# Last cross attention: a mask bias over 32 rows per group, and four heads exponentiated by ScalarE straight from the scores

## The chip, the cores and the metric

The kernel runs on one core of a Trainium2 chip. The metric is the device time of the whole program in microseconds (us); the kernel before has a median of 1068.53 us over 3 runs (1067.91 to 1072.55). Five engines work side by side, each in its own program order: TensorE (PE, matmuls and transposes; PEld is its weight load), VectorE (DVE), ScalarE (ACT), GpSimd (POOL) and SyncE (SP, which issues transfers). They meet in semaphores.

## The reference

A decoder of four layers, each a gated cross attention on 77 context tokens followed by a gated feed-forward part. The input x is 4 batches of 512 tokens of width 128; every cross attention has 16 heads. The change touches the cross attention of layer 3:

```python
qh = _rope((q @ w_q + b_q) split into 16 heads of 8)
kh = _rope((k @ w_k + b_k) split into 16 heads of 8)
vh = (v @ w_v + b_v) split into 16 heads of 8
scores = jnp.einsum('bhqd,bhkd->bhqk', qh, kh) / math.sqrt(dk)
scores = jnp.where(mask, scores, jnp.finfo(scores.dtype).min)   # mask: (4, 1, 1, 77)
attn = jax.nn.softmax(scores, axis=-1)
out = jnp.einsum('bhqk,bhkd->bhqd', attn, vh)
x = x + jnp.tanh(g_xattn[3]) * (out merged @ w_o + b_o)
```

## The kernel before

The 2048 tokens are 16 tiles of 128 (NT = 16, four tiles TB of each batch). For a tile of the last cross attention (called X3 in the code) the scores of all heads are 128 x 1232 (16 heads of 77 keys). They stand in four PSUM banks, four heads (GK = 308 columns) each: RG = 4 groups, and group g uses rows 32g to 32g+31 of the queries and of a block-diagonal key matrix, so a score matmul has 32 rows.

Each engine runs a loop over the tiles with an order written out by hand: `skewed_loop(engine, steps, ...)` runs the steps once for each k, a step with lag j being about tile k - j. For X3, in this order:

- PE: `score(k)`, `late_fold(k)` (for the first tiles only), `product(k-3)`, `turn_probs(k-2)`.
- ACT: `stage(k+1)` (copies the tile's queries to `qs`), `evacuate(k-3)` (four copies of the transposed probabilities from PSUM to `PT`), `exponent(k-1)`. As `exponent` is one tile ahead of PE's turning and `evacuate` is written before it, the exponentials of tile t stand behind the copies of tile t-2.
- DVE: `largest(k)` (maximum of each head, read from the scores), `shift(k)` (scores less the maximum, to `att`), `total(k-1)` (sum of each head), `invert(k-1)`, `update(k-3)` (adds the result to x).
- POOL: `normalize(k)` (probabilities times the reciprocal of the sum), which PE turns in `turn_probs`.

`score(k)` writes the scores in the same four banks for every tile. It waits for `staged` (ACT has copied the queries) and for `shifted` (DVE has read the scores of tile k-1 for the last time). In X3 four more matmuls add the mask's bias `nb3` to the scores: each multiplies the 128 x 128 identity `identb` with the group's 308 columns. The four tiles of a batch share the bias, and all 128 rows of it are alike. The exponential applies the scale 1/sqrt(8).

The second cross attention (X1) already has a split: there ACT takes six heads one by one (line 1349, input from SBUF, with the maximum as bias and the sum as accumulated output) and ten heads in one instruction (line 1352).

Of the kernel before, what the change touches and what calls it, by code (L numbers as in the profile page):

```python
# [6 lines left out]
BF16 = mybir.dt.bfloat16  # L7
# [3 lines left out]
ALU = mybir.AluOpType  # L11
# [5 lines left out]
KEYS = 77  # L17
H, HD = 16, 8
HD2 = 64
P = 128  # L20
# [185 lines left out]
def build(nc, x_in, packed, w_ffn1, w_moe, w_mla, split2, w_ffn3, rope, mask1, mask3, normed1, sums1, out):  # L206
    ctx = ExitStack()
    with ctx:
# [28 lines left out]
        mask3_u8 = sb("mask3_u8", [P, CK], U8)  # L237
        identb = sb("identb", [P, P], BF16)
        cmaskb = sb("cmaskb", [P, HK], BF16)
        tg = sb("tg", [P, 8])  # L240
        stats = sb("stats", [P, NT, 6])
        mv = sb("mv", [P, NT, 2])
# [212 lines left out]
        def over_group_keys(a):  # L455
            return a.rearrange("p (g h) -> p g h", g=RG).unsqueeze(3).to_broadcast([P, RG, H // RG, KEYS])

        SPLIT = H - 6

        def over_keys(a):  # L460

            return a.unsqueeze(2).to_broadcast([P, H, KEYS])

        def over_part(a):
            return a.unsqueeze(2).to_broadcast([P, SPLIT, KEYS])

        def fold_of(u):

# [128 lines left out]
        def _(pe):  # L597
# [124 lines left out]
            def cross(s):  # L722


                n0 = tiles_before(s)

                def score(t):
                    pe.wait_ge(staged, t.n + n0 + 1)

                    if s in (X1, X2):  # L730
                        pe.wait_ge(scores_read, t.n + (LAYER[s] - 1) * NT + 1)
                    else:
                        pe.wait_ge(shifted, t.n + n0 + 1)
                    causal = s == X2 and t.k % TB == 0
                    if s == X2:
                        for c in range(3):
                            a, z = c * BANK, min((c + 1) * BANK, HK)
                            m = mm(flat[:, a:z], qs[:, t.slot(2), :], batch(KBD, t.group)[:, a:z],
                                   start=True, stop=not causal)
                            if causal:  # L740
                                m = mm(flat[:, a:z], identb[:, :], cmaskb[:, a:z], start=False, stop=True)
                    else:
                        for g in range(RG):
                            rows = slice(32 * g, 32 * g + 32)
                            m = mm(ps[:, g, 0:GK], qs[rows, t.slot(2), :], batch(KBG, t.group)[rows, :],
                                   start=True, stop=s != X3)
                        if s == X3:
                            for g in range(RG):
                                m = mm(ps[:, g, 0:GK], identb[:, :], batch(nb3, t.group)[:, g * GK:(g + 1) * GK],
                                       start=False, stop=True)  # L750
                    m.then_inc(scores, 1)

                def turn_probs(t):
                    pe.wait_ge(probs, t.n + n0 + 3)
                    if isinstance(t.n, int) and t.n == 0 and s in FOLD:
                        pe.wait_ge(vw_sb, (FOLD[s] + 1) * B + 1)
                    if s == X1 and t.n == 0:
                        pe.wait_ge(turned_sb, TURN0[X1] + 2 * B + 1)
                    for k in range(3):

                        pe.wait_ge(probsT, t.n * 3 + 3 * n0 + k + 1)
                        if s == X0 and k == 1 and 1 <= t.n <= 2 * PARTS:
                            pe.wait_ge(side_sb, side_piece(t.n - 1) + 1)
                        for c in range(4 * k, min(4 * k + 4, NC)):
                            m = P if c < NC - 1 else LAST
                            q = pe.transpose(ps[0:m, (3 if s == X2 else 4) + k, (c % 4) * P:(c % 4 + 1) * P],  # L766
                                             att[:, 2 + t.slot(2), c * P:c * P + m], ident)
                        q.then_inc(probsT_ps, 1)

                def late_fold(t):  # L770
                    if s == X1 and t.n + 2 < B:
                        turn_q1(t.n + 2)
                    if s == X3 and t.n == 0:
                        rotate(B - 1)
                        pe.wait_ge(roped, B - 1)
                        pe.wait_ge(q_sb, 2 * B)
                    if s == X3 and t.n + 2 < B:
                        fold_values(s, w(f"{LAYER[s]}wo"), t.n + 2)

                def product(t):  # L780

                    if s == X0 and t.n in (0, 2 * TB, 3 * TB):
                        pe.wait_ge(side_sb, side_piece(PARTS * (t.n // TB - 1) - 1) + 1 if t.n else side_query(3) + 1)
                    if s == X1 and t.n == 0:
                        pe.wait_ge(values_in, 16 * len(SHARES))
                    if s == X3 and t.n == 0:
                        pe.wait_ge(roped, B)
                    pe.wait_ge(x_new, t.n + XNEW0[s] - (1 if s == X2 else 0))
                    for k in range(3):
                        pe.wait_ge(probsT, t.n * 3 + 3 * n0 + k + 4)  # L790
                        for c in range(4 * k, min(4 * k + 4, NC)):
                            m = P if c < NC - 1 else LAST
                            q = mm(attended(s, t), PT[0:m, t.slot(2), c, :],  # L793
                                   batch(VW, t.group)[0:m, c * D:(c + 1) * D], start=(c == 0), stop=(c == NC - 1))
                    q.then_inc(attn_out, 1)

                if s != X2:
                    pe.wait_ge(kbd, KEYED[s] + 1)
                if s == X2:
                    pe.wait_ge(vw_bo, 1)  # L800
                elif s == X3:
                    pe.wait_ge(vw_sb, FOLD[s] * B + 3)
                if s == X2:
                    pe.wait_ge(bf_done, 2)
                if s == X3:
                    pe.wait_ge(tables_set, 4)
                if s == X0:
                    return score, product, turn_probs
                skewed_loop(pe, [(score, 0), (late_fold, 0), (product, 3), (turn_probs, 2)], NT, TB if s == X2 else NT)
# [459 lines left out]
        def _(act):  # L1269
# [58 lines left out]
            def cross(s, scale):  # L1328
# [4 lines left out]
                def stage(t):  # L1333

                    act.wait_ge(scores, t.n + n0 + 1)
                    q = FT[:, bass.ds(t.n * P, P)]
                    if s == X1:
                        go(qs[:, t.slot(2), :], q, ACT.Copy, scale=HD ** -0.5).then_inc(staged, 1)
                    else:
                        go(qs[:, t.slot(2), :], q, ACT.Copy).then_inc(staged, 1)  # L1340

                def exponent(t):
                    if s == X1:
                        act.wait_ge(rowmax, t.n + n0 + 1)
                        act.wait_ge(probsT_ps, t.n * 3 + 3 * n0 + 3)
                        wait(act, recip, t.n + n0 - 1)
                        for h in range(SPLIT, H):
                            keys = slice(h * KEYS, (h + 1) * KEYS)
                            go(att[:, 2 + t.slot(2), keys], att[:, t.slot(2), keys], ACT.Exp,
                               bias=mx[:, t.slot(2), h:h + 1], accum_out=rs[:, t.slot(2), h:h + 1])  # L1350
                        act.wait_ge(shifted, t.n + n0 + 2)
                        go(att[:, 2 + t.slot(2), 0:SPLIT * KEYS], att[:, t.slot(2), 0:SPLIT * KEYS], ACT.Exp)\  # L1352
                            .then_inc(expd, 1)
                        return
                    act.wait_ge(shifted, t.n + n0 + 2)

                    act.wait_ge(probsT_ps, t.n * 3 + 3 * n0 + 3)
                    go(att[:, 2 + t.slot(2), :], att[:, t.slot(2), :], ACT.Exp, scale=scale).then_inc(expd, 1)  # L1358
# [389 lines left out]
        def _(pool):  # L1748
# [218 lines left out]
            for b in range(B):  # L1967
                tt(heads(VBD3_at[b]), v3_s[:, b * KEYS:(b + 1) * KEYS].unsqueeze(1).to_broadcast([P, H, KEYS]),
                   over_keys(w("hm")), ALU.mult).then_inc(vbd, 1)
            pool.wait_ge(ld["e"], 32)  # L1970
            for b in range(B):
                t = pool.tensor_scalar(heads(nb3[:, b, :]),
                                       mask3_u8[:, b * KEYS:(b + 1) * KEYS].unsqueeze(1).to_broadcast([P, H, KEYS]),
# [14 lines left out]
        def _(dve):  # L1988
# [88 lines left out]
            def cross(s):  # L2077
# [14 lines left out]
                def largest(t):  # L2092
# [7 lines left out]
                    top = mx[:, t.slot(2), :]  # L2100
                    if s not in (X1, X2):
                        top = top.rearrange("p (g h) -> p g h", g=RG)
                    v.tensor_reduce(top, src, AX.X, ALU.max, negate=s == X1).then_inc(rowmax, 1)

                def shift(t):

                    a = heads(att[:, t.slot(2), :])
                    dve.wait_ge(rowmax, t.n + n0 + 1)
                    if s == X1:
                        tt(a[:, 0:SPLIT, :], a[:, 0:SPLIT, :], over_part(mx[:, t.slot(2), 0:SPLIT]), ALU.add).then_inc(shifted, 1)  # L2110
                    elif s == X2:
                        tt(a, a, over_keys(mx[:, t.slot(2), :]), ALU.subtract).then_inc(shifted, 1)  # L2112
                    else:
# [2 lines left out]

                def total(t):
                    dve.wait_ge(expd, t.n + n0 + 3)
                    n = SPLIT if s == X1 else H
                    v.tensor_reduce(rs[:, t.slot(2), 0:n], heads(att[:, 2 + t.slot(2), :])[:, 0:n, :], AX.X, ALU.add)\  # L2120
                        .then_inc(rowsum, 1)

# [710 lines left out]
```

## Time and profile before

| | before |
|---|---|
| median of 3 runs | 1068.53 us |
| profiled execution, its own time | 1071.78 us |
| its span, first to last instruction | 1069.7 us |
| PE busy over the span | 927.7 us (87%) |
| DVE busy over the span | 785.9 us (73%) |
| ACT busy over the span | 556.0 us (52%) |
| POOL busy over the span | 489.7 us (46%) |
| first score matmul of X3 | at 932.84 us |
| last update of x in X3 | at 1024.86 us |

The tile loop of X3 thus takes some 92 us of the 1069.7. Times within the program are us from the start of the span. A number in brackets at the end of a timeline row is the time in which the engine sat idle before the row, with what released it.

### The profile page before, as it was taken

How to read it: one execution, taken by the hardware profiler on the slowest of the kernel's cores; microseconds unless marked ns; L12 is line 12 of the kernel's file. 1: busy time of each engine (PE TensorE's matmuls, PEld its weight loads, DVE VectorE, ACT ScalarE, POOL GpSimd, SP SyncE). 2: the span in 40 equal slices, each digit the busy share in tenths (PEclk: the TensorE clock that was granted, in tenths of full speed). 3: DMA queues.
4: the chain of work that ended last, by engine and by line, in shares of the span. 5: the costliest groups of instructions: out<-in, count | busy, mean ns of one | idle time of the engine just before them, and what ended most of it. 6: DMA issues, size and time to landing. Idle time of an engine off the chain costs nothing.

```text
span 1069.7 us, 19683 instructions
## 1 busy us (share of the span) xinstructions
PE 927.7 (87%) x6397; PEld 663.6 (62%) x6401; DVE 785.9 (73%) x2080; ACT 556.0 (52%) x1493; POOL 489.7 (46%) x451
## 2 busy tenths in 40 slices
PE   6998985988778999859997598988989999989987
PEld 4787633767577989737775243434447677667773
DVE  5889999999756777769996476776834644589962
ACT  3675456886434445724443166666764333455523
POOL 6444553555066565625566766574530600034420
PEclk9999896999889999979999568999999999999989
DMA  9300000000211111410000322122002000000001
GB/s 326 141 1 1 2 6 1 1 1 1 41 38 41 33 44 34 119 54 1 0 1 15 98 71 84 50 83 57 23 12 88 1 1 2 1 1 1 1 1 39
DMA packets 29828, 40.55 MB, mean 38 GB/s; under 512 B 11468, under 2 KB 25036, under 8 KB 29228
## 3 DMA queue, kind: packets, MB, share of 16 engines
q1 hardware_dynamic: 27244, 34.28, 10.3%
q0 software_dynamic: 2496, 5.16, 1.9%
q8 instruction: 48, 0.79, 0.3%
q14 instruction: 40, 0.33, 0.1%
HBM read 31.44 MB, written 7.82 MB: 37 GB/s over the span
## 4 chain that ended last, share of the span: by engine, by line
PE 26%; issue 14%; POOL 7%; DVE 5%; ACT 3%; SPq 1%; DMA 0%; POOLq 0%; DVEq 0%; ACTq 0%
POOL att L1783 5%; PE ps L829 4%; PE ps L1163 4%; PE ps L819 4%; PE ps L1135 3%; PE ps L1147 3%; PE ps L793 1%; SPq L570 1%; PE ps L1249 1%; PE ps L1256 1%; DVE rs L2120 1%; PE ps L1101 0%; DVE stats L1997 0%; PE ps L607 0%; PE ps L1263 0%
## 5 line engine op out<-in xcount | busy, mean ns | idle before, releaser
L1783 POOL TENSOR_TENSOR att<-att,ri 128x1232 f32<-128x1232 f32 x64 | 169.3, 2645 | 192.4 <-DVE ri L2126 192.4
L793 PE MATMUL ps<-VW,PT 128*128 128x128 f32 (+3 forms) x1280 | 159.1, 280 | 16.6 <-DVE x L2141 15.1
L793 PEld LDWEIGHTS ps<-VW,PT 128*128 128x128 f32 (+1 forms) x1280 | 149.9, 193 | 34.7 <-DVE x L2141 27.0
L1366 ACT ACTIVATE PT<-ps 128x512 f32<-128x512 f32 x128 | 70.5, 594 | 90.0 <-PE ps L766 89.2
L766 PE MATMUL ps<-W,att 128*128 128x128 f32 (+1 forms) x640 | 87.2, 283 | 16.8 <-POOL att L1783 15.3
L1757 POOL TENSOR_TENSOR rstd<-ve,minus_half 128x4 f32<-128x4 f32 x38 | 38.9, 1040 | 114.1 <-DVE ve L2012 97.5
L900 PE MATMUL ps<-PT,att 128*128 128x128 f32 x624 | 79.9, 283 | 9.9 <-issue 9.0
L766 PEld LDWEIGHTS ps<-W,att 128*128 128x128 f32 (+1 forms) x640 | 73.0, 143 | 22.9 <-POOL att L1783 16.1
L829 PEld LDWEIGHTS ps<-U,att 128*128 128x128 f32 x512 | 66.3, 191 | 33.1 <-issue 29.1
L2577 DVE CUSTOM_DVE_ANT_0 C<-ps,cmaskb 128x512 bf16<-128x512 f32 (+1 forms) x128 | 71.1, 555 | 20.2 <-PE ps L1135 17.4
L2577 DVE CUSTOM_DVE_ANT_0 U<-ps,cmaskb 128x384 bf16<-128x384 f32 (+1 forms) x128 | 54.0, 422 | 43.1 <-PE ps L1135 42.9
L2120 DVE TENSOR_REDUCE rs<-att 128x16 f32<-128x1232 f32 (+1 forms) x64 | 83.6, 1306 | 1.2 <-ACT att L1352 0.8
L900 PEld LDWEIGHTS ps<-PT,att 128*128 128x128 f32 x624 | 75.0, 197 | 14.0 <-issue 12.8
L1135 PE MATMUL ps<-W,U 72*128 72x512 bf16 (+3 forms) x256 | 68.7, 344 | 16.4 <-DMA W<-split 9.5
L2273 DVE SCALAR_TENSOR_TENSOR U<-ps,w_all,U 128x128 f32<-128x128 f32 x128 | 36.0, 344 | 57.1 <-PE ps L829 57.0
L1414 ACT ACTIVATE att<-ps 128x512 f32<-128x512 f32 x64 | 38.1, 597 | 74.9 <-PE ps L819 74.9
L1147 PE MATMUL ps<-U,W 108*128 108x512 bf16 (+3 forms) x256 | 72.3, 323 | 5.4 <-ACT VW L1672 2.1
L1358 ACT ACTIVATE att<-att 128x1232 f32<-128x1232 f32 x48 | 59.2, 1234 | 33.5 <-DVE att L2112 33.5
L829 PE MATMUL ps<-U,att 128*128 128x128 f32 x512 | 67.6, 276 | 3.1 <-DVE U L2273 2.4
L819 PE MATMUL ps<-FT,U 128*128 128x512 f32 x128 | 65.0, 595 | 0.0
L1440 ACT ACTIVATE FT<-ps,att 128x128 f32<-128x128 f32 x156 | 44.7, 375 | 35.2 <-PE ps L900 29.1
L1840 POOL DMA_INDIRECT PT<-normed,VBD x39 | 42.0, 1078 | 40.0 <-DVE VBD L2376 28.5
(430 smaller groups left out, 2120.6 us busy)
## 6 DMA issues: line engine op xcount, KB each, us to landing
U<-in_ffn SPq DMA_DIRECT2D x1, 6176.0 KB, 23.4
U<-split SPq DMA_DIRECT2D x144, 32.0 KB
W<-split SPq DMA_DIRECT2D x144, 32.0 KB
W<-in_packed SPq DMA_DIRECT2D x1, 2162.5 KB, 23.9
U<-in_ffn SPq DMA_DIRECT2D x1, 2060.0 KB, 9.5
U<-in_moe SPq DMA_DIRECT2D x1, 2048.0 KB, 7.4
split<-VBD SPq DMA_DIRECT2D x4, 384.0 KB, 2.9
split<-W SPq DMA_DIRECT2D x4, 384.0 KB, 2.8
```

What stands on the lines that cost most here:

```text
L766: q = pe.transpose(ps[0:m, (3 if s == X2 else 4) + k, (c % 4) * P:(c % 4 + 1) * P], att[:, 2 + t.slot(2), c * P:c * P + m], ident)
L793: q = mm(attended(s, t), PT[0:m, t.slot(2), c, :], batch(VW, t.group)[0:m, c * D:(c + 1) * D], start=(c == 0), stop=(c == NC - 1))
L819: mm(ps[:, u % 2, :], W1M[:, e, j * P:(j + 1) * P], FT[:, cols(c)], start=True, stop=True)\
L829: t = mm(ps[:, 4 + e % 2, i * D:(i + 1) * D], hh[:, u % 2, i * P:(i + 1) * P], W2M[:, e, j, :], start=(j == 0 and i == 0), stop=(j == J2 - ...
L900: t = mm(ps[:, 2 + 2 * k + a, c * P:(c + 1) * P], chosen1[:, k, at:at + P], pickedT[:, k, :], start=True, stop=True)
L1135: mm(ps[:, 2 * (t % RINGS), 0:(i + 1) * P], queries[0:STACK, n % HOLD, g, i * P:(i + 1) * P], keys[0:STACK, n % HOLD, g, 0:(i + 1) * P], s ...
L1147: mm(ps[:, 2 * (t % RINGS) + 1, 0:S - j * P], keys[0:rows, n % HOLD, g, j * P:(j + 1) * P], queries[0:rows, n % HOLD, g, j * P:S], start=T ...
L1358: go(att[:, 2 + t.slot(2), :], att[:, t.slot(2), :], ACT.Exp, scale=scale).then_inc(expd, 1)
L1366: go(PT[:, t.slot(2), 4 * k:4 * k + 4, :].rearrange("p c n -> p (c n)"), ps[:, k0 + k, :], ACT.Copy).then_inc(probsT, 1)
L1783: tt(p, p, over_keys(ri[:, t.slot(2), :]), ALU.mult).then_inc(probs, 1)
L2120: v.tensor_reduce(rs[:, t.slot(2), 0:n], heads(att[:, 2 + t.slot(2), :])[:, 0:n, :], AX.X, ALU.add)\
L2577: v.tensor_tensor_reduce(unused[t % 2][:, 0:z], ps[:, 2 * (t % RINGS), 0:z], visible[:, S - z:S], -1.0, -NEG, ALU.add, ALU.min, nm[:, n % ...
```

## The change

There are two parts. First, the mask's bias: the stationary operand is no longer the identity but 32 rows of a constant `part_ones` (all elements 1/32), against the same 32 rows of the bias; the sum of 32 equal rows over 32 is the bias. POOL sets the constant once, before the loop.

Second, the exponentials: ACT scales the queries when it stages them and no longer in the exponential. DVE takes the maximum negated, as in X1, and shifts three groups (12 heads, 924 columns). The last four heads, which are the whole of bank 3, are exponentiated by ACT one by one from PSUM, with the maximum as bias and the sum accumulated; DVE sums only 12 heads. As ACT now reads scores, the next tile's `score` waits for it as well (`scores_read`).

```diff
-        SPLIT = H - 6
+        SPLIT = {X1: H - 6, X3: H - H // RG}
...
                     else:
                         pe.wait_ge(shifted, t.n + n0 + 1)
+                        if s == X3:
+                            pe.wait_ge(scores_read, t.n + (LAYER[s] - 1) * NT + 1)
...
                             for g in range(RG):
-                                m = mm(ps[:, g, 0:GK], identb[:, :], batch(nb3, t.group)[:, g * GK:(g + 1) * GK],
-                                       start=False, stop=True)
+                                rows = slice(32 * g, 32 * g + 32)
+                                m = mm(ps[:, g, 0:GK], part_ones[rows, :],
+                                       batch(nb3, t.group)[rows, g * GK:(g + 1) * GK], start=False, stop=True)
...
-                    if s == X1:
+                    if s in (X1, X3):
                         go(qs[:, t.slot(2), :], q, ACT.Copy, scale=HD ** -0.5).then_inc(staged, 1)
...
                 def exponent(t):
-                    if s == X1:
+                    if s in SPLIT:
                         act.wait_ge(rowmax, t.n + n0 + 1)
                         act.wait_ge(probsT_ps, t.n * 3 + 3 * n0 + 3)
                         wait(act, recip, t.n + n0 - 1)
-                        for h in range(SPLIT, H):
+                        n = SPLIT[s]
+                        for h in range(n, H):
                             keys = slice(h * KEYS, (h + 1) * KEYS)
-                            go(att[:, 2 + t.slot(2), keys], att[:, t.slot(2), keys], ACT.Exp,
-                               bias=mx[:, t.slot(2), h:h + 1], accum_out=rs[:, t.slot(2), h:h + 1])
+                            own = slice((h - n) * KEYS, (h - n + 1) * KEYS)
+                            e = go(att[:, 2 + t.slot(2), keys], att[:, t.slot(2), keys] if s == X1 else ps[:, RG - 1, own],
+                                   ACT.Exp, bias=mx[:, t.slot(2), h:h + 1], accum_out=rs[:, t.slot(2), h:h + 1])
+                        if s == X3:
+                            e.then_inc(scores_read, 1)
                         act.wait_ge(shifted, t.n + n0 + 2)
-                        go(att[:, 2 + t.slot(2), 0:SPLIT * KEYS], att[:, t.slot(2), 0:SPLIT * KEYS], ACT.Exp)\
-                            .then_inc(expd, 1)
+                        go(att[:, 2 + t.slot(2), 0:n * KEYS], att[:, t.slot(2), 0:n * KEYS], ACT.Exp).then_inc(expd, 1)
                         return
...
             pool.wait_ge(ld["e"], 32)
+            pool.memset(part_ones[:, :], 1.0 / 32).then_inc(zeros_set, 1)
+            pool.wait_ge(zeros_set, B + 4)
...
-                    v.tensor_reduce(top, src, AX.X, ALU.max, negate=s == X1).then_inc(rowmax, 1)
+                    v.tensor_reduce(top, src, AX.X, ALU.max, negate=s in SPLIT).then_inc(rowmax, 1)
...
+                    elif s == X3:
+                        g = RG - 1
+                        m = mx[:, t.slot(2), 0:SPLIT[s]].rearrange("p (g h) -> p g h", g=g).unsqueeze(3)
+                        tt(by_group(att[:, t.slot(2), :])[:, 0:g], group_scores(s)[:, 0:g],
+                           m.to_broadcast([P, g, H // RG, KEYS]), ALU.add).then_inc(shifted, 1)
...
-                    n = SPLIT if s == X1 else H
+                    n = SPLIT.get(s, H)
```

ACT's queue in the X3 loop, one turn before (`PT` are the copies of `evacuate`, `att` the exponential, lines 1369 and 1370 its last two copies; the bracket names the semaphores that a row waits for):

```order
L1364 REGISTER_ALU [waits attn_out]
L1366 ACTIVATE PT<-ps 128x512 [waits probsT_ps]
L1364 REGISTER_ALU
L1366 ACTIVATE PT<-ps 128x512 [waits probsT_ps]
L1364 REGISTER_ALU
L1369 ACTIVATE PT<-ps 128x128 [waits probsT_ps]
L1370 ACTIVATE PT<-ps 80x128
L1357 ISA [waits shifted]
L1358 ACTIVATE att<-att 128x1232 [waits probsT_ps]
```

The same turn now:

```order
L1371 REGISTER_ALU [waits attn_out]
L1373 ACTIVATE PT<-ps 128x512 [waits probsT_ps]
L1371 REGISTER_ALU
L1373 ACTIVATE PT<-ps 128x512 [waits probsT_ps]
L1371 REGISTER_ALU
L1376 ACTIVATE PT<-ps 128x128 [waits probsT_ps]
L1377 ACTIVATE PT<-ps 80x128
L1349 ISA [waits rowmax]
L1355 ACTIVATE att,rs<-ps,mx 128x77 [waits recip,probsT_ps]
L1355 ACTIVATE att,rs<-ps,mx 128x77 x3
L1360 ACTIVATE att<-att 128x924 [waits shifted]
```

The four copies stay ahead; between them and the large exponential stand four exponentials that read the scores from PSUM.

PE's queue at the end of the turning and the start of the next tile's scores, before (`KBD,qs` are the score matmuls, `C,identb` the mask's, `VW,PT` the product):

```order
L766 MATMUL ps<-W,att 128x128 [waits probsT]
L766 MATMUL ps<-W,att 80x128
L745 MATMUL ps<-KBD,qs 128x308 [waits shifted,q_staged]
L745 MATMUL ps<-KBD,qs 128x308 x3
L749 MATMUL ps<-C,identb 128x308 x4
L793 MATMUL ps<-VW,PT 128x128 [waits probsT,x_new]
```

And now:

```order
L770 MATMUL ps<-W,att 128x128 [waits probsT]
L770 MATMUL ps<-W,att 80x128
L748 MATMUL ps<-KBD,qs 128x308 [waits scores_read,shifted,q_staged]
L748 MATMUL ps<-KBD,qs 128x308 x3
L753 MATMUL ps<-C,part_ones 128x308 x4
L797 MATMUL ps<-VW,PT 128x128 [waits probsT,x_new]
```

Nothing changes place on PE; the first score matmul has one more semaphore to wait for, and the mask's matmuls another stationary operand.

## Rows read from the trace of the kernel before

**Rows 1.** Window: length; busy (x count) of PE, PEld, DVE, ACT, POOL; PE clock.
```profile
951.00:1012.00 61.00, 59.68 (x523) 49.28 (x522) 57.78 (x62) 32.30 (x71) 27.01 (x12) 1.00 0.01 2
```
**Rows 2.** Timeline of X3's loop, two tiles: start us, duration us, engine, line, what.
```profile
974.74 0.25 DVE L2126 RECIPROCAL ri<-rs 128x16 f32<-128x16 f32 x1
975.07 2.25 POOL L1783 TENSOR_TENSOR att<-att,ri 128x1232 f32<-128x1232 f32 x1 [2.98 <-DVE ri L2126]
...
978.79 0.80 PE L745 MATMUL ps<-KBD,qs 32*128 32x308 f32 x8
...
979.52 0.70 PE L749 MATMUL ps<-C,identb 128*128 128x308 bf16 x4
979.53 1.24 ACT L1358 ACTIVATE att<-att 128x1232 f32<-128x1232 f32 x1
...
980.06 2.39 PE L793 MATMUL ps<-VW,PT 128*128 128x128 f32 x20
980.26 1.44 DVE L2103 TENSOR_REDUCE mx<-ps 128x16 f32<-128x1232 f32 x1 [0.37 <-PE ps L749]
...
981.74 1.44 DVE L2114 TENSOR_TENSOR att<-ps,mx 128x1232 f32<-128x1232 f32 x1
...
982.29 1.26 PE L766 MATMUL ps<-W,att 128*128 128x128 f32 x10
...
983.10 1.43 DVE L2120 TENSOR_REDUCE rs<-att 128x16 f32<-128x1232 f32 x1
...
983.48 0.80 PE L745 MATMUL ps<-KBD,qs 32*128 32x308 f32 x8
...
984.56 0.25 DVE L2126 RECIPROCAL ri<-rs 128x16 f32<-128x16 f32 x1
```
**Rows 3.** Groups by line and form, DVE of X3, ACT of X1.
```profile
L2114 DVE TENSOR_TENSOR att<-ps,mx 128x1232 f32<-128x1232 f32 x16 | 23.1, 1441 | 0.5
...
L2120 DVE TENSOR_REDUCE rs<-att 128x16 f32<-128x1232 f32 x16 | 22.8, 1426 | 0.0
...
L1349 ACT ACTIVATE att<-att,mx 128x77 f32<-128x77 f32 x96 | 33.1, 358 | 0.0
L1349 ACT ACTIVATION_READ_ACCUMULATOR att<-att,mx 128x1 f32 x96 | 19.2, 200 | 0.0
```
**Rows 4.** Timeline of ACT in X1: first of six heads, and what follows the sixth.
```profile
194.83 0.36 ACT L1349 ACTIVATE att<-att,mx 128x77 f32<-128x77 f32 x1
...
196.89 0.84 ACT L1352 ACTIVATE att<-att 128x770 f32<-128x770 f32 x1
```
**Rows 5.** Timeline of PE in the third cross attention: scores over 128 rows.
```profile
493.22 2.23 PE L738 MATMUL ps<-KBD,qs 128*128 x6
495.29 0.94 PE L793 MATMUL ps<-VW,PT 128*128 x7
```
**Rows 6.** Timeline of X3: score of tiles 1, 3 and 15, first exponential, last update.
```profile
937.52 0.80 PE L745 MATMUL ps<-KBD,qs 32*128 32x308 f32 x8
...
939.11 1.24 ACT L1358 ACTIVATE att<-att 128x1232 f32<-128x1232 f32 x1
...
948.63 1.32 PE L745 MATMUL ps<-KBD,qs 32*128 32x308 f32 x8
...
1008.35 0.80 PE L745 MATMUL ps<-KBD,qs 32*128 32x308 f32 x8
...
1024.86 0.35 DVE L2141 SCALAR_TENSOR_TENSOR x<-ps,tg,x 128x128 f32<-128x128 f32 x1 [2.00 <-PE ps L793]
```
**Rows 7.** Timeline of PE after two idle stretches of over 2 us.
```profile
472.99 2.34 PE L738 MATMUL ps<-KBD,qs 128*128 128x512 f32 x6 [2.59 <-ACT qs L1340]
...
946.30 2.40 PE L766 MATMUL ps<-W,att 128*128 128x128 f32 x10 [2.43 <-POOL att L1783]
```
**Rows 8.** Windows of PE: us, busy (x count), granted clock, DMA.
```profile
946.00:950.00 4.00, 3.70 (x19) 0.57 0.00 0
...
474.00:478.00 4.00, 1.33 (x5) 1.00 0.00 0
```

More of the change, by code:

```diff
@@ L239, in build @@
         cmaskb = sb("cmaskb", [P, HK], BF16)
+        part_ones = sb("part_ones", [P, P], BF16)
         tg = sb("tg", [P, 8])
@@ L464, in over_part @@
         def over_part(a):
-            return a.unsqueeze(2).to_broadcast([P, SPLIT, KEYS])
+            return a.unsqueeze(2).to_broadcast([P, SPLIT[X1], KEYS])
         def fold_of(u):
@@ L2109, in shift @@
                     if s == X1:
-                        tt(a[:, 0:SPLIT, :], a[:, 0:SPLIT, :], over_part(mx[:, t.slot(2), 0:SPLIT]), ALU.add).then_inc(shifted, 1)
+                        n = SPLIT[s]
+                        tt(a[:, 0:n, :], a[:, 0:n, :], over_part(mx[:, t.slot(2), 0:n]), ALU.add).then_inc(shifted, 1)
+                    elif s == X3:
[3 more added lines that the diff above has]
+                           m.to_broadcast([P, g, H // RG, KEYS]), ALU.add).then_inc(shifted, 1)
                     elif s == X2:
```

## Prediction

> **What bounds the kernel now.** I first read the windows over X3's tile loop. The reader is to see there that two engines are nearly full: in 61 us PE is busy 59.68 and DVE 57.78, while ACT has 32.30 and POOL 27.01, and PE's clock is 1.00, the 2.4 GHz level [rows 1]. So DVE time taken away gives something only if PE can go faster too, and an idle stretch put into PE's queue costs nearly its full length.
>
> The second view is the timeline of the loop [rows 2]. PE's turn (scores, mask, product of tile k-3, turning of tile k-2) has no wait between 978.79 and 983.48: 4.69 us, PE's floor. DVE's strand takes two tiles: invert at 974.74, POOL's normalize at 975.07, the turning, scores at 978.79, mask at 979.52, maximum at 980.26, shift at 981.74, sum at 983.10, invert again at 984.56. That is 9.82 us for two tiles, 4.91 each. From the score of tile 3 at 948.63 to that of tile 15 at 1008.35 there are 12 turns in 59.72 us, 4.98 each [rows 6]: now PE is the last, now the strand.
>
> The third thing is ACT's place. When the next score starts at 978.79, the turning is over; ACT finishes its four copies of the turned tile and starts its exponential only at 979.53, 0.74 us later [rows 2]. Before, no score waited for that: `score` waited for DVE's shift, done long before.
>
> **The change part by part.**
>
> *The four heads' exponentials and the new wait.* In X1 six such exponentials take from 194.83 to 196.89, 0.343 us each from start to start, with the reading of the accumulator inside [rows 4]. Four of them: three steps of 0.343 and the last one's own 0.358 [rows 3], 1.39 us. They stand behind the copies, and `score` of the next tile waits for the last of them. A turn of PE thus gets a tail that nothing hides, since PE is in order and the product and the turning stand behind the waiting score: 0.74 for the copies, 1.39 for the heads, and a handover. For that the rows show 0.08 from the reciprocal's end (974.99) to POOL's start (975.07) and 0.04 from the mask's end to the maximum; I take 0.1. The tail is 2.23 us.
> These exponentials read PSUM, which no row of before shows with an accumulator. Bounds: from below the element rate of the whole exponential, 1.24 us for 1232 columns [rows 2], 0.31 for 308; from above four times exponential and accumulator one after the other, 4 x (0.358 + 0.200) = 2.23 [rows 3]. I take 1.39, as it is the same instruction with another source.
> The Trainium skill, "ScalarE: Activation LUTs", section "Rules for kernel authors", budgets about 0.3 us per ACTIVATE and 0.83 ns per element: an estimate from that page is 0.364 us for a head and 1.46 for four; the X1 rows say 0.343 and 1.37. By the page the end would be 0.07 x 13, about 1 us later.
>
> *The mask over 32 rows per group.* The mask's phase is 979.52 to 980.06, 0.54 us [rows 2]. What four row groups side by side are worth, scores show: the third cross attention streams 2 x 1232 columns through all rows in 2.07 us (493.22 to 495.29) [rows 5], X3 the same 2 x 1232 columns over 32 rows per group in 0.73 (978.79 to 979.52) [rows 2], a factor of 2.8. So the mask goes to 0.19, a gain of 0.35. Bounds: no gain at all, and 0.54 / 4 = 0.135, a gain of 0.41.
>
> *DVE's work.* Shift and sum have 924 instead of 1232 columns: 1441 and 1426 ns [rows 3] become about 1080 and 1070 in proportion, gains of 0.36 each per tile. Bounds: nothing, and all of it on the path, 0.72 x 16 = 11.5 us. In the loop I cost them at nothing, as DVE then waits for PE.
>
> *The rest.* The scale in ACT's staging and the negated maximum are in instructions that run anyway. The constant is one memset of 128 columns on POOL ahead of the loop; POOL is half idle there. Nothing, at most 1 us.
>
> **The new turn.** PE's work is 4.69 - 0.35 = 4.34, and the tail 2.23: 6.57 us. The tail closes a ring: score(k), product, turning of k-2, copies of k-2, heads of k, score(k+1). No buffer opens it, for the scores of all tiles share four banks. The other ring, DVE's strand, becomes 9.82 + 2.23 - 0.35 - 0.72 = 11.0 for two tiles, 5.5 each, and is hidden.
>
> **The sum.**
> - Beginning: the score of tile 1 started at 937.52. Now it waits for the heads of tile 0, which start where the exponential started, 939.11 [rows 6]: 939.11 + 1.39 + 0.10 = 940.60, +3.1. From there to the score of tile 3 the way leads over the maximum, shift, sum, normalize and turning of tile 0, and then the tail: + 2.23 - 0.35 - 0.72, and - 1.14 because I book the slow clock below (2.40 for ten transposes at 946.30 [rows 7] against 1.26 at 982.29 [rows 2]). That is 0. Together +3.1.
> - Tiles 3 to 15: 12 x 6.57 = 78.8 instead of 59.7: +19.1.
> - End: from 1008.35 to 1024.86 [rows 6] DVE's strand ends it. It gets shorter by 0.35 (mask), 0.36 (shift) and two sums (0.72), and I give 0.2 back for the last tile's exponentials, which now come after the heads: -1.2.
> - Sum at the fast clock: +21.0.
> - Clock: PE now has some 14 idle stretches of about 2.2 us. The rows show both outcomes for such a stretch: after 2.43 us at 946.30 the clock was at 0.57 over the next 4 us, and after 2.59 us at 472.99 it stayed at 1.00 [rows 7, 8]. At 0.57, 3.4 of the 4 us are at 1.2 GHz, half of which is lost: 1.7 us for a fall. I take one stretch in four: 3.5 x 1.7 = +6.
>
> That is +27. The profiled execution had 1071.78 us (span 1069.7 and 2.1 around it); it becomes 1099. It stood 3.25 above the median of the runs, so I forecast 1096 us.
>
> **The rivals.**
> - *B: the clock falls in most turns.* Mechanism: a turn idles a third of the time, so PE slips to 1.2 GHz after nearly every tail. For it: the fall at 946.30 [rows 7]. Against it: the 472.99 row. If each of 14 falls costs 1.7, the sum is 21 + 24 = 45, 1114 us; if they last longer than one piece of work, 1125 and more. The Trainium skill, "TensorE: Matmul & The Clock Gate", section "A second HAM failure mode: psum-queue depth-cycling", describes a kernel in which small idle times between bursts make the clock go up and down all the time; by that rule B is the case, and the traces so far show falls here and there only.
> - *C: the tail is shorter.* If the four exponentials from PSUM run near the element rate (0.31 us instead of 1.39), the turn is 5.5 us, where DVE's ring stands as well: 12 x 0.5 at the tiles, 2 at the beginning, -1 at the end, and few falls: +7 to +12, 1076 to 1081 us. Against it: 0.343 in every X1 tile.
> - *D: faster.* The ring would not close if the heads ended no later than the turning: then their start would have to be 1.5 us before the next score and not 0.74 behind it. From that point on the gains decide: PE's floor 4.34, DVE's strand 9.82 - 0.35 - 0.72 = 8.75 for two, 4.4 a turn; 12 x (4.98 - 4.4) = 7, and 1 at the end: 1060.5. For it is that DVE is 95% busy. Against it: the copies stand in front of the heads in ACT's queue, and they need the turning.
> - *E: the mask alone misses.* With no gain from it, A has 0.35 x 13 = 4.6 more: 1101. It is inside A's range.
>
> **How the numbers follow.** A, the tail with some falls: 0.66, its own range 1087 to 1104 (no fall 1089.5; mask and heads as bounded nearby). B 0.17, C 0.11, D 0.04, and 0.02 for an end within 0.5% of before (5.3 us, what a measurement of this kernel can hardly tell from no change), which needs C and a tail that mostly hides. The range of 1080 to 1117 holds A, the better end of B and the worse end of C. Faster 0.04, same 0.02, slower 0.94.
>
> **What would show it.** In the trace of the changed kernel: PE's score rows of X3 released by ACT (the exponential of one head from PSUM), with some 2.2 us idle before most of them; 6.6 us from score to score; the heads 0.34 apart, and the first 0.74 behind the turning's end; mask phase 0.2; shift near 1.08, sum near 1.07, and a DVE that now waits over 2 us a tile for the mask; the clock at half in a few stretches. The forecast is wrong if scores start right behind the turning (D), if the heads' rows are closer than 0.3 apart (C), or if the transposes of most tiles take 2.4 instead of 1.26 us (B). X1, X2 and all stages ahead of X3 should be as before; a difference there would be another cause.

## The result, and the profile after

The changed kernel takes 1101.25 us in the median of 5 runs (1100.50 to 1102.83), beside 1068.87 us for the kernel before (5 runs). The ratio is 1.0298, with a 95% interval of 1.0275 to 1.0320: about 3% slower, 32.4 us in the medians. The profiled execution took 1100.5 us with a span of 1098.5, 28.8 more than the span before; the execution profiled before had been 2.9 us above its median, which is most of the difference between 28.8 and 32.4.

The page's first part is of little help: PE has 930.1 us (85%) busy now, DVE 775.2 (71%), ACT 572.5 (52%). Work hardly changed. The tile loop of X3 shows what did. First the window that answers to [rows 1] (the same columns), here over the loop and over its undisturbed middle:

```profile
951.00:1038.00 87.00, 59.17 (x514) 50.35 (x512) 51.66 (x64) 47.98 (x180) 28.70 (x13) 0.94 0.00 1
975.00:1012.00 37.00, 24.30 (x232) 20.74 (x233) 21.29 (x26) 21.94 (x83) 13.09 (x6) 1.00 0.00 1
```

PE was busy 98% of the loop and DVE 95%; now each is below 70% of it (24.30 and 21.29 of 37 us in the middle). A loop in which no engine is full must be held by waits, and the waits view (waiting engine and line, releaser: total us, times, longest) names them:

```profile
DVE mx L2112 <- PE ps L753: 38.1, 13, 5.4
ACT PT L1373 <- PE ps L770: 34.2, 14, 4.1
...
PE ps L748 <- ACT att L1355: 27.8, 13, 2.2
```

PE's scores wait for ACT's last head in every turn, ACT for PE's turning, DVE for the scores. The timeline of one turn, which answers to [rows 2] (start, duration, engine, line; in brackets the idle time and its releaser), shows the order of the joints:

```profile
996.78 0.80 PE L748 MATMUL ps<-KBD,qs 32*128 32x308 f32 x8 [2.14 <-ACT att L1355]
...
997.37 0.34 PE L753 MATMUL ps<-C,part_ones 32*128 32x308 bf16 x4
...
997.64 2.50 PE L797 MATMUL ps<-VW,PT 128*128 128x128 f32 x20
997.75 1.44 DVE L2112 TENSOR_REDUCE mx<-ps 128x16 f32<-128x1232 f32 x1 [2.46 <-PE ps L753]
...
999.23 1.12 DVE L2124 TENSOR_TENSOR att<-ps,mx 128x924 f32<-128x924 f32 x1
...
999.98 1.26 PE L770 MATMUL ps<-W,att 128*128 128x128 f32 x10
...
1000.61 1.08 ACT L1373 ACTIVATE PT<-ps 128x512 f32<-128x512 f32 x2 [2.45 <-PE ps L770]
...
1001.74 0.28 ACT L1377 ACTIVATE PT<-ps 80x128 f32<-80x128 f32 x1
1001.90 0.33 ACT L1355 ACTIVATE att<-ps,mx 128x77 f32<-128x77 f32 x1
...
1002.80 0.34 ACT L1355 ACTIVATE att<-ps,mx 128x77 f32<-128x77 f32 x1
1003.00 0.22 ACT L1355 ACTIVATION_READ_ACCUMULATOR att<-ps,mx 128x1 f32 x1
1003.10 0.99 ACT L1360 ACTIVATE att<-att 128x924 f32<-128x924 f32 x1
...
1003.37 0.80 PE L748 MATMUL ps<-KBD,qs 32*128 32x308 f32 x8 [2.14 <-ACT att L1355]
```

From score to score it is 6.59 us. The last copy of the turned tile (1001.74), the first head (1001.90), the fourth (1002.80) and the next score (1003.37) stand one after the other. DVE finished with these scores at 1000.35, the end of its shift, 3 us before the next score began. The granted clock answers to [rows 8] (windows of PE, same columns):

```profile
930.00:948.00 18.00, 12.23 (x74) 0.81 0.00 1
948.00:975.00 27.00, 20.27 (x148) 0.81 0.00 1
975.00:1012.00 37.00, 24.30 (x232) 1.00 0.00 1
1012.00:1022.00 10.00, 7.86 (x61) 0.83 0.01 2
1022.00:1038.00 16.00, 9.52 (x94) 1.00 0.00 0
```

A mean of 0.81 is a clock at its lower level, 1.2 GHz, for 38% of the stretch. In all it stood there for some 20 us of X3, against some 3.4 us before [rows 8]. Single turns show it: the six turns from 977.00 to 1016.56 take 6.59 to 6.60 us each, but three turns of the loop take 8.2, 8.1 and 8.2 us, such as this one, whose scores begin at the lower clock (1.41 instead of 0.80 us):

```profile
1016.56 1.41 PE L748 MATMUL ps<-KBD,qs 32*128 32x308 f32 x8 [2.14 <-ACT att L1355]
1017.72 0.51 PE L753 MATMUL ps<-C,part_ones 32*128 32x308 bf16 x4
1018.15 3.32 PE L797 MATMUL ps<-VW,PT 128*128 128x128 f32 x20
1021.31 1.26 PE L770 MATMUL ps<-W,att 128*128 128x128 f32 x10
1024.71 0.80 PE L748 MATMUL ps<-KBD,qs 32*128 32x308 f32 x8 [2.14 <-ACT att L1355]
```

The groups that answer to [rows 3], with busy us, mean ns and idle us before them:

```profile
L2124 DVE TENSOR_TENSOR att<-ps,mx 128x924 f32<-128x924 f32 x16 | 17.9, 1120 | 0.5
L2135 DVE TENSOR_REDUCE rs<-att 128x12 f32<-128x924 f32 x16 | 17.7, 1106 | 0.2 <-ACT att L1360 0.2
...
L1355 ACT ACTIVATE att<-ps,mx 128x77 f32<-128x77 f32 x64 | 19.8, 336 | 0.0
L1355 ACT ACTIVATION_READ_ACCUMULATOR att<-ps,mx 128x1 f32 x64 | 14.0, 219 | 0.0
```

DVE did get its relief (1441 and 1426 ns before). Between tile 3 and tile 15 PE never waits for DVE any more, so there the relief is worth nothing; only the end of X3, where DVE's work is the path, gets it.

Cut along X3, in us, from the two traces:

| stretch | before | after | difference |
|---|---|---|---|
| start to the score of tile 0 | 932.85 | 931.40 | -1.5 |
| score of tile 0 to that of tile 3 | 15.78 | 22.70 | +6.9 |
| tile 3 to tile 15 (12 turns) | 59.72 | 83.86 | +24.1 |
| tile 15 to the last update of x | 16.51 | 15.32 | -1.2 |
| from there to the end | 44.84 | 45.22 | +0.4 |
| span | 1069.7 | 1098.5 | +28.8 |

The first row is no effect that can be told from the spread: in the two later traces of the changed kernel the score of tile 0 starts at 937.12 and 930.70, so the part ahead of X3 differs by 6 us between executions of the same kernel.

### The profile page after: what moved, and what is told of

Read it like the earlier page. It is cut to its first block, busy times and chain, and to the rows that moved or that the text cites. A ratio compares the mean times of both kernels' runs of the same rounds, so it can differ in the third digit from the quotient of the medians.

```text
span 1098.5 us, 19828 instructions
## 1 busy us (share of the span) xinstructions
PE 930.1 (85%) x6401; PEld 667.0 (61%) x6401; DVE 775.2 (71%) x2080; ACT 572.5 (52%) x1621; POOL 488.7 (44%) x452
## 4 chain that ended last, share of the span: by engine, by line
PE 35%; issue 8%; POOL 6%; ACT 6%; DVE 3%; SPq 1%; DMA 0%; ACTq 0%; POOLq 0%; DVEq 0%
PE ps L833 5%; PE ps L823 5%; PE ps L1167 4%; PE ps L797 4%; POOL att L1790 4%; PE ps L1139 4%; PE ps L1151 3%; ACT att L1355 2%; PE ps L748 1%; PE ps L673 1%; PE ps L770 1%; PE ps L1260 1%; PE ps L1253 1%; ACT PT L1373 1%; PE ps L608 0%
## 5 line engine op out<-in xcount | busy, mean ns | idle before, releaser
L797 PE MATMUL ps<-VW,PT 128*128 128x128 f32 (+3 forms) x1280 | 162.7, 284 | 14.7 <-DVE x L2156 12.6
L797 PEld LDWEIGHTS ps<-VW,PT 128*128 128x128 f32 (+1 forms) x1280 | 152.8, 196 | 35.9 <-DVE x L2156 23.3
L770 PEld LDWEIGHTS ps<-W,att 128*128 128x128 f32 (+1 forms) x640 | 72.4, 142 | 20.9 <-POOL att L1790 13.3
L2112 DVE TENSOR_REDUCE mx<-ps 128x16 f32<-128x1232 f32 x32 | 46.1, 1441 | 55.1 <-PE ps L753 43.7
L2135 DVE TENSOR_REDUCE rs<-att 128x16 f32<-128x1232 f32 (+2 forms) x64 | 78.5, 1226 | 1.4 <-ACT att L1360 1.0
L1421 ACT ACTIVATE att<-ps 128x512 f32<-128x512 f32 x64 | 38.1, 597 | 76.6 <-PE ps L823 76.6
L748 PE MATMUL ps<-KBD,qs 32*128 32x308 f32 x384 | 43.9, 530 | 35.1 <-ACT att L1355 33.8
```

Source lines behind the costliest of these rows:

```text
L797: q = mm(attended(s, t), PT[0:m, t.slot(2), c, :], batch(VW, t.group)[0:m, c * D:(c + 1) * D], start=(c == 0), stop=(c == NC - 1))
```

## The experiments

My theory had three parts: the loss is the wait of `score` for ACT's heads, which puts copies, heads and PE's turn in series; the rest of it is the clock, which PE's idle stretches pull down; and the mask part is a gain. The rivals: ACT's longer queue or reading PSUM costs the time wherever it stands; the clock's falls are hidden by the ring; the mask's form costs something or is hidden.

The kernel before has another median in each group of runs measured together (1059.91, 1069.70 and 1073.50 us), so whole times are compared as ratios to the runs of before beside them. The finer measures, both from each trace, are the mean turn of tiles 3 to 15 and the stretch from the first score of X3 to the last update of x.

| kernel | ratio to before, 95% interval | mean turn | X3, first score to last update |
|---|---|---|---|
| before | 1 | 4.98 | 92.0 |
| the changed kernel | 1.0298 (1.0275 to 1.0320) | 6.99 | 121.9 |
| mask alone | 0.9973 (0.9954 to 0.9993) | 4.82 | 89.6 |
| heads before the copies | 1.0179 (1.0141 to 1.0217) | 6.16 | 113.1 |
| PE filled | 1.0221 (1.0182 to 1.0259) | 6.51 | 112.9 |
| heads from SBUF, mask | 0.9937 (0.9911 to 0.9963) | 4.62 | 85.6 |
| the changed kernel, second time | 1.0294 (1.0252 to 1.0337) | 6.99 | 122.0 |
| heads from PSUM alone | 1.0294 (1.0250 to 1.0339) | 7.30 | 128.4 |
| heads from SBUF, old mask | 0.9959 (0.9942 to 0.9977) | 4.83 | 89.2 |
| six heads from SBUF, mask | 0.9931 (0.9906 to 0.9956) | 4.51 | 84.3 |
| the changed kernel, third time | 1.0265 (1.0234 to 1.0296) | 6.99 | 122.0 |
| heads from PSUM alone, again | 1.0293 (1.0252 to 1.0334) | 7.04 | 119.4 |

**The mask alone** (e1): the kernel before with

```diff
-                                m = mm(ps[:, g, 0:GK], identb[:, :], batch(nb3, t.group)[:, g * GK:(g + 1) * GK],
+                                rows = slice(32 * g, 32 * g + 32)
+                                m = mm(ps[:, g, 0:GK], part_ones[rows, :],
+                                       batch(nb3, t.group)[rows, g * GK:(g + 1) * GK], start=False, stop=True)
```

Expected: 

> The kernel before with the mask's bias over 32 rows per group alone; the exponentials stay as before. In the trace after, score and mask phases together take 0.86 us instead of 1.27. My theory (the loss comes wholly from the wait for ACT's heads; the mask part is a gain) expects DVE's two-tile strand to shrink by about 0.4, a turn of 4.7 to 4.8 us instead of 4.98, and 3 us less than before: 1065 to 1067 us. The rival that the mask's new form costs something (a slower or later matmul over 32 rows) expects 1070 us or more.

Measured: 1056.28 us against 1059.91, 2.9 us less by the ratio, with an interval that excludes 1. A turn took 4.82 us. The mask part is a gain, as the prediction had it, and the rival that it costs something is out.

**The heads before the copies** (e3): in ACT's list of steps

```diff
-                    steps = [(stage_last, -1), (evacuate, 3), (exponent, 1), (late_fold, 0)]
+                    steps = [(stage_last, -1), (last_heads, 1), (evacuate, 3), (exponent, 1), (late_fold, 0)]
```

`last_heads` being the four exponentials taken out of `exponent`.

Expected: 

> The changed kernel with ACT's four exponentials of heads from PSUM put ahead of the four copies of evacuate (they still wait for the turning of tile t-2, whose buffer they write). My theory (a ring PE - copies - heads - next score, each link in series) expects the tail of 2.2 us to lose the copies' 0.6 to 0.7 us, a turn of about 5.9 instead of 6.6 us, and 8 to 10 us less than the changed kernel: 1091 to 1093 us. The rival that the price lies in the exponentials' own length or in reading PSUM beside DVE expects no change: 1101 us.

Measured: the ratio is 1.0179. Against the changed kernel's three ratios (1.0265 to 1.0298) that is 9 to 13 us less; the changed kernel ran in other groups, so X3 is the closer measure, and it is 8.8 us shorter. PE's idle time before a score, from the timeline:

```profile
980.94 0.33 ACT L1354 ACTIVATE att<-ps,mx 128x77 f32<-128x77 f32 x1 [2.30 <-PE ps L770]
...
981.85 0.33 ACT L1354 ACTIVATE att<-ps,mx 128x77 f32<-128x77 f32 x1
...
982.15 1.09 ACT L1390 ACTIVATE PT<-ps 128x512 f32<-128x512 f32 x2
...
982.42 0.80 PE L748 MATMUL ps<-KBD,qs 32*128 32x308 f32 x8 [1.52 <-ACT att L1354]
```

It is 1.52 instead of 2.14 us: the copies' share is gone from the tail. The turns are 5.96 to 6.14 us after the first, 6.02 in the mean, 0.58 less than the undisturbed 6.60 and near the expected 5.9. Over 12 turns that is 7.0 us; another 3.0 us of the loop are clock, as only one turn was long and not three; and the end became 1.2 us longer. The same exponentials, with the same source and the same number, cost less when they stand elsewhere. So it is the place in the queue that counts; the rival (no change) falls.

**PE filled** (e4): between the two waits of `score` in X3

```diff
                         pe.wait_ge(shifted, t.n + n0 + 1)
                         if s == X3:
+                            for _ in range(32):
+                                mm(ps[:, 0, 0:P], identb[:, :], identb[:, :], start=True, stop=True)
                             pe.wait_ge(scores_read, t.n + (LAYER[s] - 1) * NT + 1)
```

Expected: 

> The changed kernel with 32 idle matmuls of 128 columns (into bank 0, whose scores DVE has read, before the wait for ACT; they add nothing to the result) in each turn of PE in X3, some 1.8 us of the 2.14 us in which PE idles. My theory says that the part of the loss beyond the ring is the clock: with PE busy it stays at 2.4 GHz in X3, every turn takes 6.6 us, none 8.1, and 6 to 9 us go: 1092 to 1095 us. If the clock's falls cost nothing (the ring hides them), the time stays at 1101; if the fill gets in the way of the scores, it is more.

Measured: 1.0221 of before. Against the changed kernel's three ratios that is 5 to 8 us less, and the interval overlaps that of the lowest of them (1.0265), so the whole program's time supports this result without settling it. In the traces X3 is 9.0 us shorter. PE's window over the whole of X3 (same columns as the windows of PE above) and two turns:

```profile
920.00:1035.00 115.00, 106.41 (x1229) 1.00 0.01 1
```

```profile
963.25 1.95 PE L737 MATMUL ps<-identb 128*128 128x128 bf16 x32
965.47 0.80 PE L750 MATMUL ps<-KBD,qs 32*128 32x308 f32 x8 [0.27 <-ACT att L1357]
...
969.76 1.95 PE L737 MATMUL ps<-identb 128*128 128x128 bf16 x32
971.98 0.80 PE L750 MATMUL ps<-KBD,qs 32*128 32x308 f32 x8 [0.27 <-ACT att L1357]
```

The clock stays at 1.00, 2.4 GHz, and every turn of the loop takes 6.5 to 6.6 us. The wait for ACT is still there, only filled. This splits the loss in two: with the clock held, X3 is still 20.9 us longer than before, and the clock is most of the other 9.0. Two side effects of the filling nearly cancel. The undisturbed turn is 0.08 us shorter, 1.0 us in all. And before the score of tile 3 the filling came late, since it waited for DVE's shift first:

```profile
937.56 1.95 PE L737 MATMUL ps<-identb 128*128 128x128 bf16 x32 [1.54 <-DVE att L2126]
937.59 0.34 ACT L1357 ACTIVATE att<-ps,mx 128x77 f32<-128x77 f32 x1
...
939.43 0.80 PE L750 MATMUL ps<-KBD,qs 32*128 32x308 f32 x8
```

The last head began at 937.59; 0.57 us behind the last head's start, as in the other turns of the changed kernel, the score could have begun at 938.16, so by this estimate the filling itself cost 1.3 us there. The clock's price is then 9.0 - 1.0 + 1.3, about 9.2 us. The changed kernel's own trace agrees: its three long turns are 4.7 us longer than three of 6.60, and its beginning 4.5 us longer than this one less the 1.3. So the rival that the waits hide the clock's price is out.

**The heads from SBUF** (e5): DVE shifts all 16 heads again, ACT's four heads read `att` without a bias, and `score` no longer waits for ACT.

```diff
-                        if s == X3:
-                            pe.wait_ge(scores_read, t.n + (LAYER[s] - 1) * NT + 1)
...
-                            e = go(att[:, 2 + t.slot(2), keys], att[:, t.slot(2), keys] if s == X1 else ps[:, RG - 1, own],
-                                   ACT.Exp, bias=mx[:, t.slot(2), h:h + 1], accum_out=rs[:, t.slot(2), h:h + 1])
+                            bias = {"bias": mx[:, t.slot(2), h:h + 1]} if s == X1 else {}
+                            go(att[:, 2 + t.slot(2), keys], att[:, t.slot(2), keys], ACT.Exp,
+                               accum_out=rs[:, t.slot(2), h:h + 1], **bias)
...
-                        tt(by_group(att[:, t.slot(2), :])[:, 0:g], group_scores(s)[:, 0:g],
-                           m.to_broadcast([P, g, H // RG, KEYS]), ALU.add).then_inc(shifted, 1)
+                        tt(by_group(att[:, t.slot(2), :]), group_scores(s), over_group_keys(mx[:, t.slot(2), :]),
+                           ALU.add).then_inc(shifted, 1)
```

Expected: 

> The changed kernel, but DVE shifts all 16 heads to SBUF as before the change and ACT's four heads read them there, so that the next score waits for DVE's shift alone; ACT does the same number of exponentials with accumulators, DVE sums 12 heads, the mask is over 32 rows. My theory (the wait on the scores' banks is what costs, not ACT's work) expects the turn to go back to PE's floor and DVE's strand, 4.5 to 4.7 us, and a time below the kernel before: 1062 to 1066 us. The rival that ACT's longer turn (four heads more, 1.2 us) sets the time whatever they read expects 1075 us or more.

Measured: 1051.61 us against 1059.91, ratio 0.9937: 0.6% faster than before, with an interval that excludes 1, and 3.2 to 3.5% faster than the changed kernel by the ratios. In the timeline the scores start with no wait, while ACT's heads run beside PE's mask and product:

```profile
970.07 0.80 PE L746 MATMUL ps<-KBD,qs 32*128 32x308 f32 x8
...
970.69 0.31 PE L751 MATMUL ps<-C,part_ones 32*128 32x308 bf16 x4
...
970.80 0.28 ACT L1355 ACTIVATE att<-att 128x77 f32<-128x77 f32 x1
...
970.93 2.50 PE L795 MATMUL ps<-VW,PT 128*128 128x128 f32 x20
...
974.45 0.80 PE L746 MATMUL ps<-KBD,qs 32*128 32x308 f32 x8
```

ACT issues as many exponentials with accumulators as in the changed kernel, and DVE does more. What is gone is the score's wait for ACT, and the whole loss with it. The rival of ACT's longer queue falls. The edit takes away the reading of PSUM and the bias at the same time, but those are small by themselves: the heads are 0.25 us apart here and 0.30 in the changed kernel, 0.2 us for four.

**The changed kernel again**, on the chip of the next three.

Expected: 

> The changed kernel once more, on the same chip as the experiments beside it, for a ratio that can be held against theirs: 1.028 to 1.032 of before.

Measured: 1.0294. Its X3 repeats the first trace turn for turn (the three long turns are at the same tiles, and X3 takes 122.0 us), although its span is 5.8 us longer (1104.3): the difference lies ahead of X3.

**The heads from PSUM alone** (e2): the changed kernel with the first diff of this section taken back.

Expected: 

> The changed kernel with the mask's bias as before (identity, 128 rows): the heads from PSUM alone. As PE's work is in series with the tail, the mask's and scores' saving of 0.4 us a turn is lost at full length: my theory expects a turn of 7.0 us and 5 to 7 us more than the changed kernel. The rival that the mask is hidden in the loop expects no difference.

Measured: an undisturbed turn is 6.90 instead of 6.60 us, where I had expected 7.0. X3 is 6.4 us longer, but only 3.7 of that lie in the 12 turns from tile 3 to tile 15, and the rest in the beginning and the end. The whole program's ratio was the changed kernel's, 1.0294, with an interval of 0.4% on both sides: the 5 to 7 us that I expected are not in it. The pair was measured a second time, with more runs.

Expected of the changed kernel: 

> The changed kernel again, with more rounds, as the measure for the run beside it: 1.028 to 1.032 of before.

Expected of the heads alone: 

> The heads from PSUM alone, mask as before, with more rounds, since the first time the trace showed turns of 6.9 us and 6.8 us more from X3's first score to the end, but the medians of the whole program did not differ from the changed kernel's. If the trace is right, the median is 4 to 7 us above the changed kernel's in the same call; if the gain of the mask is lost elsewhere in the program, they are equal again.

Measured: 1.0265, just under what I had expected, and 1.0293, some 3 us more. The intervals overlap widely, so on the whole program the mask's gain in this place is not shown. The changed kernel's six times lie between 1098.0 and 1102.3, those of the heads alone in two groups, 1096.2 to 1098.7 and 1106.1 to 1108.4; the four times of each from the first measurement show no such picture (1097.1 to 1106.3 and 1095.9 to 1109.0). The first trace of the heads alone has a span of 1107.1 us, the second one of 1094.2. Of these 12.9 us 9.0 lie in X3 (128.4 and 119.4), and there the clock differs:

```profile
930.00:948.00 18.00, 11.15 (x93) 1.00 0.01 1
948.00:1038.00 90.00, 62.98 (x543) 0.98 0.00 1
```

That is the shorter one; the longer one has 0.81 over the first 18 us of X3, 0.94 over the next 60 and 0.89 over the 32 after them. Both have the same undisturbed turn, here in the shorter one:

```profile
978.50 0.80 PE L747 MATMUL ps<-KBD,qs 32*128 32x308 f32 x8 [2.14 <-ACT att L1353]
...
985.40 0.80 PE L747 MATMUL ps<-KBD,qs 32*128 32x308 f32 x8 [2.14 <-ACT att L1353]
```

So in series with the tail the mask's 0.3 us a turn shows in every undisturbed turn, and in one of two traces the clock gave more than that back: its X3 is 2.6 us shorter than the changed kernel's. How often it does is not settled; two traces are no frequency.

**The sums on ACT without the mask part** (e6) and **six heads** (e7): e5 with the old mask, and e5 with `X3: H - 6`.

Expected: 

> The version with four heads on ACT from SBUF (all heads shifted by DVE), with the mask's bias as before: ACT's sums alone. It takes 0.32 us of DVE's two-tile strand: a turn of 4.8 us, PE's floor being 4.69, so 1 to 3 us less than before, and 4 to 5 us more than with the mask over 32 rows. If the gain of the SBUF version came from the mask alone, it is equal to before.

Expected: 

> Six heads instead of four on ACT from SBUF, mask over 32 rows. DVE's sum loses another 0.16 us, ACT's turn grows by 0.5 to about 4.3 us, just below PE's floor of 4.4. I expect 0 to 1 us less than the version with four; if ACT becomes the last link, the turn is over 4.6 us and the time 1 to 4 us more.

Measured: e6 1065.72 us against 1069.70, ratio 0.9959, some 4 us less where I had expected 1 to 3; its turns are 4.69 to 4.90 after the first. Moving four sums to ACT is worth something by itself. The distance to e5 is 2.3 us by the ratios, not the 4 to 5 that I had expected for the mask, and the intervals overlap; in the traces X3 is 3.6 us longer than in e5. e7 1062.84 us, ratio 0.9931; its turns are 4.38 to 4.55 after the first; 4.38 is also the shortest turn in e5, where PE did not wait. It cannot be told from four heads by its ratio (0.9937), although its X3 is 1.2 us shorter in the traces. Both versions with heads from SBUF and the new mask beat the kernel before and the changed one.

## Why the prediction was right

The forecast was 1096 us, 27 more than before, with a range of 1080 to 1117; measured are 1101.25, 32.4 more. The case that I called A is what the trace shows, and the experiments bear out its mechanism: put the heads ahead of the copies, and the turn shortens by what the copies took; take the score's wait for ACT away, and the loss is gone. Step by step:

- **The tail.** Forecast 2.23 us, from turning to next score; measured 2.20: PE starts the transposes at 999.98, which take 1.19 where work follows them [rows 2], and the next score at 1003.37. That it fits so well is luck in part, since two errors cancel. The heads are 0.30 us apart and not 0.343, so that the four take 1.24 to the end of the last one, not 1.39; the handover is 0.23 from that end to the score, not 0.1.
- **PE's work in a turn.** Forecast 4.34; measured 4.39. Scores and mask took 0.86 us and not 0.92, the product 2.34 and not 2.23.
- **The turn.** Forecast 6.57, measured 6.60 at the full clock: +19.4 for 12 turns, forecast +19.1.
- **The end.** -1.2, as forecast, and on the path that was forecast: scores and mask give 0.50 there, one shift and two sums 0.95, and the last exponential comes 0.26 later behind the heads.
- **The beginning.** Forecast +3.1 at the full clock. Measured +6.9 with the falls in it. With PE filled, where the clock never fell, it is +3.6, of which the filling itself cost 1.3, so some +2.4. The path was only in part the forecast one. I had the score of tile 1 wait for the heads of tile 0, and left out that the score of tile 2 waits in the same way for those of tile 1: in the changed kernel POOL had normalized tile 0 by 946.83, but PE came to turn it only behind that score, which started at 948.22. In both waits the heads stand behind ACT's four copies of the folded values and one staging, and PE idles 2.99 us and not 2.2.
- **DVE at nothing in the loop.** Right: it waits 38.1 us for the mask in the loop.
- **The clock.** This is the term that was mis-sized. I took one idle stretch in four, 3.5 falls of 3.4 us, some 12 us at the lower level and +6. The trace has some 20 us at that level in X3, and their price is about 9 us: 4.7 in the three long turns and 4.5 in the beginning. The share of one in four was a guess between two rows, and that it came as near as this is luck. Rival B, a fall after nearly every tail, did not come: the scores from 977.00 to 1009.97, six in a row, ran at 1.00 with 2.14 us idle before each.
- **The sum.** At the full clock +2.4, +19.4 and -1.2 make 20.6, forecast 21.0; with the clock's 9.2 it is 29.8, against 29.9 measured for X3 and a forecast of 27.
- **C and D.** C's condition, heads nearer than 0.3 us, was just missed. C's price had a flaw: I let DVE's ring stand at 5.5 us there, but that figure has the long tail in it; with the short one it is 4.95, and PE alone makes the turn of 5.5. D's condition did not occur: the heads started 0.73 us behind the turning.
- **E.** The mask did not miss: alone it is a gain of 0.3% (e1), although its own phase gave 0.27 us and not 0.35; the scores gave another 0.13.

From profiled execution to profiled execution the difference is 28.8 us, 1.8 more than my sum. The other 3.6 of the 5.4 us lie in the reference: the execution profiled before stood 2.9 us above its median and the one after 0.75 below it, while I took them to stand alike.

## What to carry to other kernels

Ask of every new reader of a shared buffer where it stands in its engine's queue, not how long it takes: here 1.2 us of exponentials, on an engine that was half idle, put 2.2 us of idle time into each turn of PE (a turn of 6.6 instead of 5.0 us), since they stood behind copies that needed the very engine which waited for them. Work can be moved to an idle engine if what frees the buffer stays with the engine that was early; the same four heads, read from the shifted copy, made the kernel 0.4% faster, and 0.6% with the mask's new form. And an idle stretch of some 2 us in each turn of PE can have a second price, the clock, which in this case was some 9 of X3's 29.9 us and which idle matmuls bought back.

## What the runs showed of the hardware

- An exponential of 77 columns with an accumulator is issued 0.343 us after the one before with its input in SBUF and a bias per partition, 0.30 with its input in PSUM and the same bias, and 0.25 with its input in SBUF and no bias (means 358, 336 and 270 ns). So with the same bias the PSUM source is 0.04 quicker (X3 of the changed kernel against X1), and with the same source the missing bias 0.09 (X3 of e5 against X1). No run had heads from PSUM without a bias, so whether the two add up is open. In e5 the last copy of the turned tile, 128 columns over 80 partitions and without an accumulator or a bias, is followed by the next instruction after 0.16 us (970.64 to 970.80).
- Over 32 rows per group, the four mask matmuls took 0.27 us from start to the next work (0.24 in e5), and 0.54 over 128 rows. The scores ahead of them ended earlier as well, 0.59 to 0.62 instead of 0.73 us, counted from their start to the mask's.
- Equal idle stretches are not followed by the same clock: in the changed kernel six of 2.14 us in a row left it at 1.00, and after the one before 1016.56 the scores ran at the lower level. Which turns are hit was the same in three traces of the changed kernel, taken at different times.
